# Graph attention: where the node one-hots of the window sums are made

## The reference

```python
q = (h @ Wq + bq).reshape(n, OUT_DIM, H) * scaling
k = (h @ Wk + bk).reshape(n, OUT_DIM, H)
v = (h @ Wv + bv).reshape(n, OUT_DIM, H)
s = jnp.einsum('edh,edh->eh', q[row], k[col])
m = jax.ops.segment_max(s, row, num_segments=n)
p = jnp.exp(s - m[row])
z = jax.ops.segment_sum(p, row, num_segments=n)
attn = p / z[row]
out = jax.ops.segment_sum(attn[:, None, :] * v[col], row, num_segments=n)
```

## Time and profile before

| | us |
|---|---|
| median of 3 runs | 2334.08 |
| lowest and highest run | 2333.65, 2336.39 |
| profiled execution, its own time | 2332.2 |
| its span | 2330.3 |
| POOL busy | 1636.8 (70%) |
| TensorE busy (matmuls) | 1670.3 (72%) |
| VectorE busy | 1539.0 (66%) |
| ScalarE busy | 435.6 (19%) |

### The profile page before, as it was taken

The page is one execution under the profiler, slowest core; times in us unless marked ns, Lnnn a source line. Parts: engine busy times, 40 slices in busy tenths (PEclk is TensorE's granted clock), DMA queues, the critical chain, the costliest instruction groups (busy, mean ns, idle before and its releaser), DMA issues. The chain is left out here.

```text
span 2330.3 us, 32319 instructions
## 1 busy us (share of the span) xinstructions
PE 1670.3 (72%) x8464; PEld 1238.1 (53%) x8464; DVE 1539.0 (66%) x5260; ACT 435.6 (19%) x994; POOL 1636.8 (70%) x1687
## 2 busy tenths in 40 slices
PE   4877777765766766775567667667957888888886
PEld 3655555553555555554444444444426667677775
DVE  8776776665666666664355555556657787788785
ACT  0000000002000000002111111111343343344342
POOL 6777777775777777775777777774227777777772
PEclk9975555555556665555587777787555555555555
DMA  5233233232233233235232332332423333333331
GB/s 139 56 85 83 57 85 84 56 84 70 56 84 84 85 84 112 56 84 155 54 98 83 98 99 83 98 99 82 80 87 107 105 108 106 108 105 107 108 104 36
DMA packets 149656, 207.12 MB, mean 89 GB/s; under 512 B 48936, under 2 KB 111387, under 8 KB 149360
## 3 DMA queue, kind: packets, MB, share of 16 engines
q0 software_dynamic: 61280, 138.20, 22.1%
q1 hardware_dynamic: 87186, 65.12, 9.5%
q10 hardware_dynamic: 1010, 1.73, 0.2%
HBM read 172.14 MB, written 36.04 MB: 89 GB/s over the span
## 5 line engine op out<-in xcount | busy, mean ns | idle before, releaser
L507 POOL DMA_INDIRECT G<-h_d,idx x832 | 794.6, 955 | 283.9 <-issue 261.8
L570 PE MATMUL p_g<-S,G 128*128 128x96 f32 (+1 forms) x2496 | 609.0, 390 | 462.6 <-DMA G<-h_d,idx 300.7
L570 PEld LDWEIGHTS p_g<-S,G 128*128 128x128 f32 x2496 | 526.6, 292 | 667.2 <-issue 295.0
L1338 POOL DMA_INDIRECT G<-kv_d,idx x416 | 432.4, 1039 | 201.8 <-issue 201.8
L507 POOL DMA_INDIRECT G<-in_x,idx x416 | 397.6, 956 | 132.2 <-issue 119.4
L928 DVE TENSOR_SCALAR work<-iota_h,key_f 128x600 bf16<-128x600 f16 x416 | 171.0, 411 | 253.9 <-PE p_d L581 253.6
L903 DVE SCALAR_TENSOR_TENSOR S<-con,rel,shared 128x96 f32<-128x96 f32 (+1 forms) x1248 | 315.4, 293 | 0.5
L581 PE MATMUL p_d<-work 128*128 128x312 bf16 (+1 forms) x832 | 272.2, 428 | 18.0 <-DVE work L943 17.1
L921 DVE TENSOR_TENSOR agg<-agg,p_g 128x96 f32 (+1 forms) x624 | 143.7, 230 | 104.1 <-PE p_g L570 84.3
L1406 PE MATMUL p_w<-S,PV 128*128 128x40 f32 x832 | 199.2, 415 | 0.7 <-DVE PV L1676 0.7
L943 DVE TENSOR_TENSOR work<-work,p_d 128x312 f32 (+1 forms) x416 | 190.8, 459 | 10.4 <-issue 9.6
(11 more groups left out here) (253 smaller groups left out, 2093.3 us busy)
## 6 DMA issues: line engine op xcount, KB each, us to landing
work<-A_d SPq DMA_DIRECT2D x25, 800.0 KB, 4.5
A_d<-work SPq DMA_DIRECT2D x12, 1600.0 KB, 7.5
G<-h_d,idx POOLq DMA_INDIRECT x832, 2.5
G<-in_x,idx POOLq DMA_INDIRECT x416, 2.5
G<-kv_d,idx POOLq DMA_INDIRECT x416, 2.8
h_d<-XH SPq DMA_DIRECT2D x75, 64.0 KB
h_d<-in_x SPq DMA_DIRECT2D x2, 1600.0 KB, 7.4
kv_d<-kv_s SPq DMA_DIRECT2D x25, 128.0 KB, 1.7
```

Of the source, the lines that this page charges most:

```text
L507: pool.indirect_dma_start(G[:, c % GRING, :], None, l.table, bass.IndirectOffsetOnAxis(ap=l.places[:, c:c + 1], axis=0)).then_inc(s_arr[g ...
L570: last = pe.matmul(p_g[:, g % PB, 0:width], G[:, c % GRING, :], S[:, c % (SRING * GR), 0:width], start=(k == 0), stop=(k == GR - 1))
L1338: pool.indirect_dma_start(G[:, c % KRING, :], None, d["kv"], bass.IndirectOffsetOnAxis(ap=idx[:, c:c + 1], axis=0)).then_inc(s_ar[c // QC ...
```

## The change

VectorE no longer compares for `S01`. ScalarE copies (and widens) the four quarters of `oh1` into `S01` instead, as `window_factors(q)`, at the end of its step, behind the last `one_hot_copy`. The copies of batch k-1 are made in step k, so `oh1` becomes a ring of four batches (OH1). VectorE's `one_hots` waits for the `S01` copies of the batch whose place it takes, instead of for `thrice`. The wait of the window sums for `s_s01` stays; it now comes from ScalarE.

```diff
@@
 QRING = 8
+OH1 = 4
@@
-    oh1 = sb("oh1", [P, 2, CB, WA], BF16)
+    oh1 = sb("oh1", [P, OH1, CB, WA], BF16)
@@
                 act.activation(ohn[:, k % 2, chunks].rearrange("p c (w s) -> p c w s", s=QR),
-                               bc(oh1[:, k % 2, chunks], 3, QR), ACT.Copy).then_inc(s_ohn, 1)
+                               bc(oh1[:, k % OH1, chunks], 3, QR), ACT.Copy).then_inc(s_ohn, 1)
+
+            def window_factors(q):
+                k, chunks = q // 4, slice(q % 4 * QC, (q % 4 + 1) * QC)
+                act.wait_ge(s_oh1, q + 1)
+                if k > 0:
+                    act.wait_ge(s_mm, q - 3)
+                act.activation(S01[:, chunks, :], oh1[:, k % OH1, chunks, :], ACT.Copy).then_inc(s_s01, 1)
@@
                         one_hot_copy(4 * k + 6)
                         one_hot_copy(4 * k + 7)
+                    if mid:
+                        for j in range(4):
+                            window_factors(4 * k - 4 + j)
@@
             def one_hots(k):
-                if k >= 2:
-                    dve.wait_ge(s_ohn, 4 * (k - 1))
+                if k >= OH1:
+                    dve.wait_ge(s_s01, 4 * (k - OH1 + 1))
                 for j in range(4):
                     c = k * CB + j * QC
-                    dve.tensor_tensor(oh1[:, k % 2, j * QC:(j + 1) * QC, :], bc(iota, 1, QC),
+                    dve.tensor_tensor(oh1[:, k % OH1, j * QC:(j + 1) * QC, :], bc(iota, 1, QC),
                                       bc(rel[:, c:c + QC], 2, WA), ALU.is_equal).then_inc(s_oh1, 1)
@@
-            def window_factors(k):
-                if k > 0:
-                    dve.wait_ge(s_mm, 4 * k)
-                for j in range(4):
-                    c = k * CB + j * QC
-                    dve.tensor_tensor(S01[:, j * QC:(j + 1) * QC, :], bc(iota, 1, QC), bc(rel[:, c:c + QC], 2, WA),
-                                      ALU.is_equal).then_inc(s_s01, 1)
@@
                     if mid:
-                        window_factors(k - 1)
                         if k > 1:
                             fade_log(k - 1)
                         values(4 * k - 4)
```

## The result

| | before | after |
|---|---|---|
| median of 8 runs, us | 2334.18 (2331.38 to 2337.52) | 2342.78 (2339.28 to 2345.07) |
| profiled execution, its own time | 2332.2 | 2345.07 |
| its span | 2330.3 | 2343.3 |
| attention: first gather to the end | 601.65 | 610.28 |
| first gather to last gather | 557.74 | 565.90 |

The kernel became slower by 8.6 us: ratio 1.0034, interval 1.0025 to 1.0043. The forecast was 5.4 us slower, 2339.5 in a range of 2333 to 2344.

A forecast was written before the change was run, and what follows sets the result against it. The TensorE-ScalarE-VectorE loop was taken as the bound. Steps 1-3 -0.2, 4-9 +2.0, 10 +1.3, 11 -1.8, 12-24 +4.3, end -0.2: together +5.4 us on the median 2334.08, 2339.5 us; range 2333 to 2344.

The forecast's parts named there:

- The reading of the bound: In most batches the TensorE-ScalarE-VectorE loop of 21.66 us bounds; POOL needs 20.0 us plus holds and follows.
- Part 2: Four ScalarE copies of 0.32 us per batch at step end; the first delays window sums, +0.33 us per node-tile batch.
- Step 10: No node tile: window sums now wait for ScalarE's last one-hot copy and the S01 copy, about +1.3 us.
- Part 3: Ring of four batches for `oh1`: VectorE waits for copies three steps old, 0 us; 2.5 KB more SBUF per partition.
- Part 1: Four compares (1.03 us) per batch leave VectorE: 0 in common batches, `al` 0.94 us earlier in steps 3 and 11.
- Value in the loop: 0: In a common batch, removing VectorE's compares gains the loop nothing: multiplies need `ps`, later VectorE work waits for a gather.
- the gain at `al` in step 3: VectorE forms `al` behind the compares there; without them it comes 0.94 us earlier.
- Step 11: Its 2.15 us of waiting for a gather are taken up by the later loop; with the copy's +0.33, about -1.8 us.
- Rival 3: Loop slips 0.33 us, compares L1602 hold a gather, later gathers come late: 23 us per batch at worst, 2365; chance 0.05.
- Rival 1: POOL is the bound after all: 0.28 us gained in each of 25 batches, -7, 2327 us; chance 0.10.
- Rival 2: Delay smaller, by copies nearer 0.20 us or more help from early `al`: +0 to +4.5 us, 2334 to 2338.6; chance 0.32.
- the forecast of the held gathers: POOL's long gathers stay two per batch, the first about 2.1 us, the second near 1.4.

The follow-up runs named there:

- addition alone: Kernel after, compares kept on VectorE into S01, ScalarE's copies into a buffer nothing reads, TensorE waiting for the copies only: 2338.53 us, ratio 1.0021 to the kernel before.
- removal alone: Kernel before with S01 compares for the first batch only and no ScalarE copies (sums wrong): 2339.49 us, ratio 1.002.
- light kernel: Kernel after without every sixteenth gather from the second ring on, products using an older row: 2338.14 us, one run.

## Why the prediction was right, and where it was not

**The reading of the bound: right, with less room than I gave it.** The TensorE-ScalarE-VectorE loop takes 21.65 us with no gather near (the last full steps on the two chips of 3028 and 2982 us), and POOL follows it through the holds: where a loop is 21.65, the holds are 1.6; where it is 21.91, they are 1.9 (addition alone). What I passed over is how little room POOL has: 0.4 us more of holds per batch turn the order over.

**Part 2, the copies: right in place, mis-sized by a fifth.** The copies take 325 ns, as worked out from the two longer ones. The window sums start 0.29 us behind the copy of L1498, not 0.36, since TensorE follows the S01 copy by 0.07 us and not by the 0.14 which I took from L1490 and L1359; against 0.03 before it is +0.26 per step, not +0.33. On 19 steps (4 to 9 and 12 to 24) that is 4.9 us instead of 6.3; these steps lost 7.9, and the 3.0 above it are the gathers'. Step 10 gave +1.23 for +1.3. The other three copies and the penalties cost nothing, as said.

**Part 3, the ring: 0, as said.** No wait of VectorE's L1613 for the copies into S01 shows.

**Part 1, the removal: here a step failed.** "Value in the loop: 0" is right for the loop alone, and the gain at `al` in step 3 was 0.91 for 0.94. The sentence that failed is "Since POOL is not the bound, 0.3 us either way leaves the sum": I priced the removal on POOL as less holding (the pair 0.17 us earlier, 0.11 less at 2070.68). The 0.17 us were read in step 15, where the pair waits for `ps`; in step 2 it came 1.00 us earlier. It became more holding, from 1.6 to 2.0 us per batch, because the multiplies catch other gathers, and with 2.0 POOL is the bound. The removal alone costs 4.1 us of the attention. It makes up for the mis-sized copy and is the rest of the loss: of the 8.6 us about one half is the copy's and the other the removal's. That 8.6 lies in the forecast of 4.7 to 9 us is so in part by luck: the copy alone gives 5.0, at its lower edge, and the rest came from a term that the sum had at nothing.

**Step 11: -0.5 instead of -1.8.** I let its wait for a gather vanish. With the addition alone this step takes 21.26 us, in the light kernel, with fewer gathers, 19.31; so the room was there and the gathers took it.

**The holds.** After the change too a gather ends some 0.8 us behind a multiply of two SBUF tiles: the one of 2.12 us at 2071.82 ends at 2073.94, the multiply at 2072.44 + 0.67 = 2073.11. So it is in general: in the six traces from the other chips 331 gathers take more than 1.15 us, and 325 of them end 0.78 to 0.86 us behind such a multiply; the other six (the thirteenth of the second batch, once in each trace) end 0.82 to 0.83 us behind the compares of L1602 (L1613 after the change), with no such multiply near. The removal's half of the loss rests on that. The Trainium skill, page "SBUF — State Buffer", section "Who interferes with whom", infers that a `tensor_tensor` leaves descriptor generation alone, since it takes only the read side; for these gathers the rows decide against it, whichever part of a gather it is that waits. Its other sentence there, that an instruction with two SBUF inputs contends with a GpSimd instruction that reads SBUF, agrees with them, since the gathers read their indices from SBUF.

**Rivals.** Rival 3 named part of it, gathers that come late behind a longer hold, but from the wrong cause: the slip of the loop by the copy. The addition alone has that slip and stays clean; the removal alone has none and shows it. Rival 1 is out: no common step is shorter than 21.65 for lack of compares. Rival 2 was right that the delay is smaller than 0.33, it is 0.26 in every common step; but not for a shorter copy, and its total of 0 to 4.5 us is missed. The forecast of the held gathers (about 2.1 and 1.4) fits in size; that there would be three, not two, I missed.

## What to carry to other kernels

Where two loops take equally long and one holds up the other, taking work off an engine can cost time: run the removal and the addition each by itself before the sum is believed. A copy handed to an idle engine has to stand where that engine idles, not behind the instruction that the next engine waits for. The chain of waits says little between equal loops; the step's period, and the same step with one loop out of the way, say which one is the bound.

## What was unexpected of the hardware

- Gathers on POOL and VectorE's multiplies of two SBUF tiles lock into one of two patterns, and stay there for ten steps and more: mostly the first and eleventh gather held (about 1.4 to 1.5 and 1.6 to 2.1 us), or the fourth, tenth and sixteenth (about 1.3 to 1.45, 2.06 to 2.66, 1.2 to 1.4). In three kernels the change from the second to the first came behind a long step (22.55 to 23.09 us).
- Which of VectorE's work holds a gather depends on what stands ahead of the multiply: over the compares L1613 with BF16 output the gather stays held to the multiply's end (1.79 to 2.12 us), beside the compares L1663 with FP32 output it was let go after 1.06 us. It is not the moment at which the multiply starts: where it starts 0.90 to 0.99 us behind the gather's start, gathers over the first compares took 2.39 to 2.49 us; where it starts after 0.88 to 0.94 us, gathers beside the second took 0.94 to 1.01. Whether the output type makes the difference is not shown.
- On two chips the kernel before took 2981.77 and 3027.66 us instead of 2334, with the gathers' packets as quick as ever (2.24 us). In the trace read above the waits are mostly for TensorE, and on both chips SyncE issues its first loads 3.0 to 3.5 us apart instead of 0.5. The cause stays open.
